# A two-layer graph network on one core: split fp32r score columns, arrays laid out transposed by the host, the last pair scaled late, and no identity products in TensorE's free time

## The reference, cut to what matters

```python
h = relu(layernorm(x))
# _gat_heads(x, adj, W, a):
Wh = einsum('bnf,hfo->bhno', x, W)
f1 = einsum('bhno,ho->bhn', Wh, a[:, :O]);  f2 = einsum('bhno,ho->bhn', Wh, a[:, O:])
e = f1[:, :, :, None] + f2[:, :, None, :]
e = where(e > 0, e, 0.01 * e);  e = where(adj > 0, e, -1e9)
out = einsum('bhnm,bhmo->bhno', softmax(e), Wh)
# layer 0
h = elu(_gat_heads(h, adj, W_heads, a_heads))      # 4 heads, 256 to 4 x 256
out = elu(_gat_heads(h, adj, W_out, a_out))        # 1024 to 256
y = relu(out @ w1 + b1) @ w2 + b2 + out
x = x + layernorm(y) * gamma + beta
# layer 1
h = relu(layernorm(x))
mi = h @ Wi.T;  mj = h @ Wj.T                      # L1_gnn_W = [Wi, Wj]
x = x + deg * (mi + b) + adj @ mj
```

## Time and profile before

| | us |
|---|---|
| median of 3 runs | 866.58 |
| the runs' spread | 865.97 to 866.79 |
| the profiled execution | 866.47 |
| its span, first to last record | 864.5 |

### The profile page before, as it was taken

How to read it: one execution, slowest core, us unless ns; L and a number is a source line. 1 busy time by engine, 2 the same in 40 slices (tenths; PEclk the granted TensorE clock), 3 DMA queues, 4 the chain that set the end, 5 groups by cost and what they waited for, 6 DMA issues and landing times. The chain is left out here.

```text
span 864.5 us, 20322 instructions
## 1 busy us (share of the span) xinstructions
PE 846.1 (98%) x6369; PEld 781.2 (90%) x6369; DVE 702.2 (81%) x2030; ACT 668.8 (77%) x1800; POOL 687.8 (80%) x941
## 2 busy tenths in 40 slices
PE   7899999999999999999999999999999999999987
PEld 4699999999999999999999999999999999999964
DVE  5987888888888888888888888888888888778575
ACT  4888978878787887878788788778878878878541
POOL 2679888888888888888888888888888888788752
PEclk9999999999999999999999999999999999999999
DMA  8100010011111011111101111100111110000001
GB/s 263 33 14 25 26 38 9 31 38 38 38 38 38 1 38 38 38 37 39 36 4 38 37 39 37 39 23 16 38 38 38 38 38 5 23 25 27 25 13 37
DMA packets 30249, 30.99 MB, mean 36 GB/s; under 512 B 1840, under 2 KB 29632, under 8 KB 30144
## 3 DMA queue, kind: packets, MB, share of 16 engines
q1 hardware_dynamic: 28848, 28.58, 11.0%
q10 hardware_dynamic: 1264, 1.12, 0.4%
q0 software_dynamic: 32, 0.00, 0.0%
HBM read 21.31 MB, written 8.39 MB: 34 GB/s over the span
## 5 line engine op out<-in xcount | busy, mean ns | idle before, releaser
L425 POOL TENSOR_TENSOR h_lo<-h2v,h_hi 128x512 fp32r<-128x512 f32 x128 | 165.3, 1293 | 47.6 <-ACT h_hi L1130 47.6
L1391 PE MATMUL ps<-gh_hi,wh_hi 128*128 128x256 f32 x512 | 152.4, 298 | 0.4 <-issue 0.4
L1391 PE MATMUL ps<-wo_hi,h_hi 128*128 128x258 f32 x512 | 150.6, 294 | 0.0
L1391 PE MATMUL ps<-wo_lo,h_hi 128*128 128x258 f32 x512 | 144.4, 282 | 0.0
L1391 PE MATMUL ps<-gh_hi,wh_lo 128*128 128x256 f32 x512 | 144.3, 282 | 0.0
L1391 PE MATMUL ps<-wo_hi,h_lo 128*128 128x258 f32 x512 | 144.1, 281 | 0.0
L1391 PE MATMUL ps<-gh_lo,wh_hi 128*128 128x256 f32 x512 | 143.6, 281 | 0.0
L679 DVE TENSOR_TENSOR gh_lo<-ps,gh_hi 128x512 fp32r<-128x512 f32 x128 | 88.3, 690 | 47.3 <-ACT gh_hi L1073 47.0
L1391 PEld LDWEIGHTS ps<-wo_lo,h_hi 128*128 128x128 f32 x512 | 97.3, 190 | 4.0
L1073 ACT ACTIVATE gh_hi<-ps 128x512 fp32r<-128x512 f32 x128 | 75.8, 594 | 32.3 <-PE ps L1391 32.1
L1084 ACT ACTIVATE h2e<-ps 128x512 f32<-128x512 f32 x128 | 75.6, 592 | 32.0 <-PE ps L1391 32.0
(11 more groups left out here) (178 smaller groups left out, 2712.8 us busy)
## 6 DMA issues: line engine op xcount, KB each, us to landing
xa<-in_x SPq DMA_DIRECT2D x32, 256.0 KB, 3.7
xr<-in_x SPq DMA_DIRECT2D x32, 256.0 KB, 2.9
out<-res SPq DMA_DIRECT2D x31, 256.0 KB, 3.2
lend<-in_L_gnn_W_heads ACTq DMA_DIRECT2D x4, 256.0 KB, 8.6
wo<-in_L_gnn_W_out SPq DMA_DIRECT2D x1, 1024.0 KB, 11.1
lend<-in_L_gnn_a_heads SPq DMA_DIRECT2D x1, 512.0 KB, 5.8
l1w_sb<-in_L_gnn_W SPq DMA_DIRECT2D x1, 512.0 KB, 10.2
lend<-in_L_gnn_w SPq DMA_DIRECT2D x2, 256.0 KB, 3.8
```

The source lines that it names most:

```text
L425: pool.tensor_tensor(h2_lo[:, u, :, :].rearrange("p c n -> p (c n)"), h2v[u % 2][:, :], h2_hi[:, u, :, :].rearrange("p c n -> p (c n)").bi ...
L1391: return pe.matmul(out_, lhs, rhs, start=start, stop=stop)
```

## The change

- **Layout.** The host hands over W_heads in two layouts (`w_heads` and the transposed `w_heads_t`), W_out too, the layer-1 weights transposed, the adjacency matrix with its transpose, and the small vectors as `cols` and `rows`. x and the output are stored by pairs. The transposes of a, of W_heads, of the adjacency matrix and of L1_gnn_W leave TensorE, and the dots leave VectorE; `heads_products` makes all four heads, and a new `out_products` the columns for W_out, both as fp32 products of 2 columns. ScalarE issues two loads, SyncE the rest.
- **Score columns.** The transposed h is split (`ht_high` on ScalarE, `ht_low` on VectorE), wa too, and `score_cols` makes eight fp32r products for four fp32 ones. `f_cols_split` starts with a sum over the two parts.
- **Last pair.** The second softmax, its transposes and copies go by graph. The variance plus epsilon of both norms is made by VectorE and GpSimd has only the power. Gamma is multiplied in ahead of the power, and the power goes into the residual; the centred rows of layer norm 3 go to the transposes unscaled, and its power is applied to mi and mj behind the products.
- **Identity products.** `warm` is gone.
- **Orders and banks.** The bank table and the lists of steps of all engines are new.

The diff, cut:

```diff
+def laid_out(x, adj, w_heads, a_heads, w_out, a_out, w1, b1, w2, b2, gamma, beta, l1w, l1b):
+    return {
+        "x": np.ascontiguousarray(x.reshape(PAIRS, 2, P, F).swapaxes(1, 2)),
+        "adj": np.ascontiguousarray(np.stack([adj, adj.T], axis=1)),
+        "w_heads": by_chunks(w_heads.swapaxes(0, 1), C),
+        "w_heads_t": np.ascontiguousarray(w_heads.transpose(2, 0, 1).reshape(C, P, H, F).transpose(1, 2, 0, 3)),
+        "w_out": by_chunks(w_out, K2),
+        "w_out_t": by_chunks(w_out.T, C),
...
+        "l1w": np.ascontiguousarray(l1w.reshape(F, 2, C, P).transpose(3, 1, 2, 0)),
+    }
...
             def first():
-                load_x(pair(0)); load_a_rows(); load_x(pair(1)); load_later_weights(); load_x(pair(2)); load_x(pair(3)); load_ffn_weights()
+                load_x(pair(0)); load_heads_t(); load_x(pair(1)); load_heads(); load_x(pair(2)); load_out_t(); load_later_weights(); load_x(pair(3))
...
+            def rstd_last(name, ve, rs, p):
+                pool.wait_ge(S[name + "_variance"], p.count(1, 1))
+                pool.tensor_tensor(rs[p.e][:, :], ve[p.e][:, :], minus_half[:, :], ALU.pow).then_inc(S[name + "_rstd"], 1)
...
+            def ht_low(p):
+                wait(dve, "ht_hi", p)
+                wait(dve, "cols_done", p, lag=1)
+                dve.tensor_tensor(ht_lo[:, :, :], ps[:, B_HT, :].rearrange("p (c n) -> p c n", c=C), ht_hi[:, :, :].bitcast(F32),
+                                  ALU.subtract).then_inc(S["ht_lo"], 1)
...
-                split_cols(("cols_copied", "rows"), p, ps[:, B_COLS, 0:COLS], f_cols[p.e][:, :],
-                           [f_split[p.e][:, k * COLS:(k + 1) * COLS] for k in range(3)])
+                dve.tensor_reduce(whole, ps[:, B_COLS, 0:2 * COLS].rearrange("p (b k m) -> p b m k", b=2, k=2), X, ALU.add).then_inc(S["cols_copied"], 1)
+                dve.wait_ge(S["cols_copied"], p.count(1, 1))
+                dve.tensor_copy(parts[0], whole).then_inc(S["rows_first"], 1)
...
+            def scale2_first(p, s):
+                dve.wait_ge(S["ffn_moments"], p.count(2, s + 1))
+                wait(dve, "x2_ready", p, lag=1)
+                dve.scalar_tensor_tensor(lt[p.e][:, s, :], y[:, s, :], b_mv[p.e][:, s, 0:1], gamma_bc, ALU.subtract, ALU.mult)\
+                   .then_inc(part_done("normal2_scaled", s), 1)
+            def residual2_last(p, s):
...
+                dve.scalar_tensor_tensor(x2[p.e][:, s, :], lt[p.e][:, s, :], b_rs[p.e][:, s:s + 1], xb[:, s, :], ALU.mult, ALU.add)\
+                   .then_inc(part_done("x2_ready", s), 1)
+            def center3_here(p, s):
...
+                dve.tensor_scalar(h3[p.e][:, s, :], x2[p.e][:, s, :], c_mv[p.e][:, s, 0:1], None, ALU.subtract).then_inc(S["h3_ready"], 1)
+            def mj_low_last(p, b):
...
+                dve.scalar_tensor_tensor(mj_lo[:, b, :], ps[:, B_M[b], F:2 * F], c_rs[p.e][:, b:b + 1], mj_hi[:, b, :].bitcast(F32),
+                                         ALU.mult, ALU.subtract).then_inc(S["mj_lo"], 1)
...
-            def ht_copy(p):
+            def ht_high(p):
...
+            def mj_high_last(p, b):
...
+                act.wait_ge(S["x2_rstd"], p.count(1, 1))
+                act.activation(mj_hi[:, b, :], ps[:, B_M[b], F:2 * F], ACT.Identity, scale=c_rs[p.e][:, b:b + 1]).then_inc(S["mj_hi"], 1)
...
             def heads_products(hd):
-                pe.wait_ge(wh_t_copied, hd + 1)
-                pe.wait_ge(a_cols_ready, 1)
+                if hd == 0:
+                    pe.wait_ge(cols_landed, 16)
+                pe.wait_ge(heads_t_in[hd // 2], 16)
...
+            def out_products(g):
+                pe.wait_ge(out_t_in, 16)
+                for k in (2 * g, 2 * g + 1):
+                    for j in range(C):
+                        last = mm(ps[:, B_WOA, 2 * k:2 * k + 2], wo_t[:, j, k * P:(k + 1) * P], ao_cols[:, :, j], j == 0, j == C - 1)
...
             def score_cols(p):
...
                 for b in range(2):
+                    nodes_b = slice(b * P, (b + 1) * P)
                     for c in range(C):
-                        last = mm(ps[:, B_COLS, b * 2 * H:(b + 1) * 2 * H], ht[p.e][:, c, b * P:(b + 1) * P],
-                                  wa[:, c, :, :].rearrange("p j h -> p (j h)"), c == 0, c == C - 1)
+                        mm(ps[:, B_COLS, b * COLS:(b + 1) * COLS], ht_hi[:, c, nodes_b], wa[:, c, :], c == 0, False)
+                        last = mm(ps[:, B_COLS, b * COLS:b * COLS + 2 * H], ht_lo[:, c, nodes_b], wa[:, c, 0:2 * H], False, c == C - 1)
...
-                hidden_by_rows(pair(31), 1); gather(pair(29)); ffn_out(pair(31)); warm(2, 0); ffn_by_rows(pair(31), 0); h3_transposes(pair(30))
-                ffn_by_rows(pair(31), 1); warm(2, 0); mixed(pair(30), 0); mixed(pair(30), 1); warm(2, 0); gather(pair(30)); warm(10, 0)
+                mixed(pair(29), 0); mixed(pair(29), 1); hidden_by_rows(pair(31), 0); hidden_by_rows(pair(31), 1); gather(pair(29)); ffn_out(pair(31))
+                ffn_by_rows(pair(31), 0); ffn_by_rows(pair(31), 1); h3_transposes(pair(30)); mixed(pair(30), 0); mixed(pair(30), 1); gather(pair(30))
```

1050 lines of the change are left out of this document (520 added, 530 removed).

## The result

The changed kernel takes 867.75 us (median of 14 runs, 867.33 to 868.45), the kernel before 866.24 us in the same comparison (14 runs, 864.59 to 866.82). The ratio is 1.0024, with a 95% interval of 1.0017 to 1.0030: slower by 1.5 us, 0.17 to 0.30%. The forecast was 865.5, faster by 1.0. The time lies inside the range, and the sign is wrong. The span of the profiled execution is 865.7 us for 864.5. The profiled execution (866.47) is of the upper group.

A forecast was written before the change was run, and what follows sets the result against it. Beginning bound by loads and a chain through all engines, middle by TensorE alone, end by the last pair's chain. Middle 0, beginning +3.7, end -4.7 sum to -1.0 on 866.47: 865.5 us, range 859.0 to 871.5.

The forecast's parts named there:

- Middle, score columns: Middle, TensorE: eight fp32r products take 0.80 us as four fp32 ones did, no change; bounds -12 to +7 us.
- rival D: Middle: fp32r weights load fast, at the bf16 rate; -12 us, 853.5 us; chance .05.
- Middle, the other engines: Middle: VectorE's extra low-part operation, 0.6 to 0.7 us a pair, stays off the path; cost 0.
- Rival E: Middle begins to wait, 0.1 to 0.3 us in each of 27 steps: +2.7 to +8, 868 to 873 us; chance .08.
- Beginning: Up to first h2: W_out's short products at half rate delay gh by 2.7, h2 by 3.5; +3.7 us in all.
- Rival B: Beginning: short products raise the clock before W_out's records, h2 1.6 us earlier than now; 860.2 us; chance .20.
- (a): End: half of mixed of pair 28 moves behind the last product by W_out, into waiting time; -1.4 us.
- (b): End: second softmax of pair 31 goes by graphs, ScalarE and VectorE working on different halves; -0.6 us.
- (c): End: pair 30's transposes go behind ffn's halves, its low part behind the add of b2; -0.6 and -0.6 us.
- (d): End: both layer norms of the last pair, add of b2 to last mixed, 7.8 us for 10.2; -2.4 us.
- End, clock: End: without identity products all 12 products of pair 31's mixed take 0.43 instead of 0.23 us; +0.9 with the gather.
- Rival C: Beginning and end: clock falls further without identity products, half rate lasting longer; +3.8 us, 871.0 us; chance .17.

## Why the prediction was wrong, point by point

- **Middle, score columns: right.** 0.81 us against 0.80, and -12 us (rival D) did not come. By the rule of the Trainium skill ("TensorE: Matmul & The Clock Gate", section "Weight-path perf modes — Fast Weight Load (FWL) and DoubleRow") the fast weight load is on for 128 weights whose type is not FP32. For fp32r weights the trace does not agree: they load in 0.19 to 0.20 us where bf16 ones take 0.10, and eight fp32r products of 16 and 8 columns take the time of eight fp32 records.
- **Middle, the other engines: the step that failed.** I had priced the middle's new order by one question only, who waits for whom, and taken 0 from slacks. No wait came: the sums of the records leave nothing for one. But the order itself has a price on TensorE, 0.09 us in the first wide product behind each group of short ones, and it went from 8 to 10 groups a step: +0.18 of the 0.19 us a step, +5 us. A group fewer or more alone changed the step by 0.05 to 0.06, since the short records give back a part. The row that shows it stood in the earlier trace rows (0.21 to the next start where a stream has 0.12), and I used it for a bound of the score columns instead of counting how often it happens. Rival E had the amount (0.1 to 0.3 us in each of 27 steps) and the wrong mechanism.
- **Beginning: mechanism right, 0.9 us too dear.** Forecast +3.7, measured +2.8. Score columns of pair 0 at 14.39 (forecast 15.0), of pair 1 at 22.21 (22.8), products for W_out at half rate (7.6 us with what lies between, 23.94 to 31.54), gh at 31.88 (32.9). Not foreseen: they also bring the rate down once it is up. From gh to h2 there are 7.8 us for the 7.5 expected, but by luck. The 0.8 for W_out's high part on ScalarE did not come, for ScalarE is idle behind it:

```profile
30.71 1.90 ACT L1104 ACTIVATE wo_hi<-wo 128x2048 fp32r<-128x2048 f32 x1
33.55 0.60 ACT L1125 ACTIVATE gh_hi<-ps 128x512 fp32r<-128x512 f32 x1 [0.94 <-PE ps L1425]
```

It waits for TensorE, whose first two gh units and the transposes between them ran at half rate (a unit 1.43 us for 0.78, the transposes 0.71 for 0.35); the forecast had only 0.2 for half rate behind the start of gh. Rival B was wrong: short products did not raise the rate.
- **End, chain: right in size, -5.5 for -5.6.** (a) and (b): the last product by W_out comes 830.99 - 824.38 = 6.6 us later, though beginning and middle had put it back by 7.8, -1.2; from it to out2 of pair 31 there are 9.1 us for 10.35, -1.3; together -2.5 where the forecast had -2.0; the first of the two is a remainder, and no trial took them apart. (c): from out2 to the add of b2 10.3 us for 10.9, -0.6 for -1.2. As an edit it is worth its term: undone by itself it made this stretch 11.6, +1.3, of which the norms gave back 0.5 (0.8 to 1.0 on the chain), so something else takes 0.7 in this stretch, and the runs leave open what. (d): 7.9 us for 10.2, -2.4 as forecast, of which the form of the norms is 1.8.
- **End, clock: wrong in sign.** Forecast +0.9, measured -1.2 (from mixed to the end) and 1.4 in the trials, against an execution of the kernel before in which the clock fell, and nothing against one in which it did not. I took the identity products for what kept the clock up. In the kernel before they did so in 23 of 84 executions, and the medians differ by 0.4 us. The later place of mixed of pair 30 does it better: 12 wide products, then 1.07 us of waiting. Rival C had nothing of that.
- **The sum.** Against the forecast's -1.0 the span shows +1.2. Against an execution of the kernel before in which the clock stayed up, beginning, middle and end give 2.8 + 5.0 - 5.4 = +2.4, where the times say 2.8. The middle is 5.0 above its term, the beginning 0.9 below, the end 2.0 below, nearly all of it the clock: +2.1. Without the miss in the middle the sign would have been right and the size far too small (-3.8 for -1.0).

What stays open: why the first wide product behind short ones costs 0.09 us more, what takes the 0.7 us between out2 and the add of b2, why the clock in the end of the kernel before falls in one execution and not in the next, and what the three long executions of the trial with the products for W_out behind gh spent.

## What to carry to other kernels

Where one engine is busy all the time, its order has a price of its own: count how often its work changes kind in a step, and read from one row what a change costs; a busy share doesn't show it, the distance between two records of a tile that comes once a step does. Keep short work together, as far as the banks that it writes are free. Look at all executions and not only at the median and one profile: two groups of times can be two states of the clock in a part of the kernel. Judge filler work by what runs at the higher rate behind it, and put real work into idle gaps first: here 18 identity products brought the first h2 1.5 us forward, and three quarters of a needed block in two gaps 2.2 (36.59 for 38.76 with the fp32 columns).

## What the runs showed of the hardware

- The first wide fp32r product behind short ones takes 0.20 us to the next start where one in a stream takes 0.12 (256 columns), and 0.31 for 0.23 (512 columns).
- Products of 2 columns, issued without a pause, do not keep TensorE's clock up: it was at the 2.4 GHz level for the score columns (0.91 us for eight) and at 1.2 GHz again behind the 16 records that followed (1.81 for eight).
- In the end of the kernel the clock was at the 1.2 GHz level in the last mixed of the profiles in which TensorE had waited 2.20, 2.57 and 4.13 us ahead of the last transposes or the last gather. With 1.96 to 1.98 us of waiting behind ten identity products it had fallen in one profile and not in two others. It stayed up in the last mixed of all nine profiles with 1.06 or 1.07 us of waiting.
- An fp32r product of 8 or 16 columns costs 0.10 us at the high level and 0.21 at the low one, the same as an fp32 record of 8 columns.
- The clock column of the page's slices and windows said 1.00 for the whole of the first 22.5 us in both kernels, while the durations show the low level there (eight score-column records take 1.71 and 1.73 us to the next start, for 0.80): for this stretch the durations decide.
